# Where the loads of a scan's first constants stand: one recurrence's start-up, re-queued

## The reference, cut to what matters

```python
xr, gate = jnp.split(x @ W_in.T, 2, axis=-1)
xc = silu(causal_conv(xr + t_emb[:, None, :]) + b_conv)
xn = layernorm(xc) * ln_g + ln_b
Bm, Cm, dt = jnp.split(xn @ W_xproj.T, 3, axis=-1)
dt = jnp.tanh(dt @ W_dt.T + b_dt) * 0.01
Ad = 1.0 + dt * -jnp.tanh(A_log)
Bd = Bm * jnp.minimum(jnp.linalg.norm(xn, axis=-1, keepdims=True), 1.0)
def step(h, inputs):                       # 1024 steps, h is 16 x 1024 per batch
    ad, bd, xt, ct = inputs
    h = jnp.clip(h * ad[:, :, None] + bd[:, :, None] * xt[:, None, :], -10.0, 10.0)
    return h, jnp.einsum('bd,bdh->bh', ct, h)
_, ys = jax.lax.scan(step, h0, ...)
x = x + (ys + D * xn) * silu(gate) @ W_out.T
x = x + attention_layer(x, cond_2048)
```

## Time and profile before

| what | us |
| --- | --- |
| median of 3 runs | 3259.34 |
| the profiled execution | 3254.8 |
| its span on the core | 3252.3 |
| VectorE busy in the span | 2189.3 |
| TensorE busy in the span | 2970.4 |
| pre-phase's last instruction on VectorE ends | about 576 |
| first step of the scan on VectorE | 651.24 |
| last step of the scan on VectorE ends | about 1730 |

### The profile page before, as it was taken

How to read it: one execution, slowest core, us unless ns; L and a number is a source line. 1 busy time by engine, 2 the same in 40 slices (tenths; PEclk the granted TensorE clock), 3 DMA queues, 4 the chain that set the end, 5 groups by cost and what they waited for, 6 DMA issues and landing times. The chain is left out here.

```text
span 3252.3 us, 55510 instructions
## 1 busy us (share of the span) xinstructions
PE 2970.4 (91%) x20298; PEld 1402.0 (43%) x20298; DVE 2189.3 (67%) x3124; ACT 1125.2 (35%) x1944; POOL 1135.5 (35%) x464
## 2 busy tenths in 40 slices
PE   6788887099999999999997899996999999999999
PEld 3455556033444444444443576664333333333334
DVE  3767675288889898988987244335777777777714
ACT  3555455011111111111111222121666666666630
POOL 0111112012333343333332111100666777777740
PEclk9888786588999999999998999997999999999999
DMA  2223425534556555555554344336424353535255
GB/s 68 110 101 129 150 104 185 129 77 108 146 144 155 143 148 149 146 150 152 147 145 162 112 150 152 124 128 180 104 75 105 97 128 89 130 92 131 85 184 173
DMA packets 249290, 421.87 MB, mean 130 GB/s; under 512 B 51832, under 2 KB 118008, under 8 KB 242760
## 3 DMA queue, kind: packets, MB, share of 16 engines
q1 hardware_dynamic: 167832, 326.81, 32.9%
q10 hardware_dynamic: 81328, 93.42, 12.4%
HBM read 258.87 MB, written 160.98 MB: 129 GB/s over the span
## 5 line engine op out<-in xcount | busy, mean ns | idle before, releaser
L734 DVE CUSTOM_DVE_ANT_0 b_h<-b_h,b_bx,b_bounds_all 128x256 f32<-128x256 f32 x2048 | 966.3, 540 | 118.0 <-PE b_bx L838 117.5
L1358 DVE TENSOR_REDUCE e_half_max<-ef_banks 128x4 f32<-128x2048 f32 x256 | 586.1, 2293 | 232.7 <-PE ef_banks L1311 232.6
L1501 POOL TENSOR_TENSOR e_pair_sum<-e_probs 128x2048 f32<-128x2048 f32 x128 | 586.8, 4584 | 263.3 <-PE ef_banks L1350 213.9
L1470 ACT ACTIVATE e_probs<-ef_banks 128x512 f32<-128x512 f32 x1024 | 556.1, 595 | 308.9 <-PE ef_banks L1325 308.7
L1325 PE MATMUL ef_banks<-e_qs,e_ks 97*128 97x512 f32 x1024 | 381.7, 452 | 4.0 <-DVE e_half_max L1358 3.6
L848 PE MATMUL b_y_psum<-b_h,b_c_weights 128*32 128x128 f32 x8224 | 339.7, 284 | 4.0 <-ACT b_y_stage L888 4.0
L838 PE MATMUL b_bx<-b_x_moving,b_b_weights 24*128 24x512 f32 x1024 | 262.4, 508 | 69.5 <-POOL b_c_weights L824 58.7
L888 ACT COPY b_y_stage<-b_y_psum 128x128 f32<-128x128 f32 x256 | 68.1, 266 | 721.7 <-PE b_y_psum L848 718.6
L768 PE MATMUL b_gate<-b_w_gate,b_x_tile 128*128 128x512 f32 x512 | 298.6, 666 | 0.0
L1325 PEld LDWEIGHTS ef_banks<-e_qs,e_ks 97*128 97x128 f32 x1024 | 154.4, 188 | 331.2 <-ACT e_probs L1470 312.7
L838 PEld LDWEIGHTS b_bx<-b_x_moving,b_b_weights 24*128 24x128 f32 x1024 | 96.8, 186 | 449.1 <-DVE b_h L734 389.1
(11 more groups left out here) (176 smaller groups left out, 3248.7 us busy)
## 6 DMA issues: line engine op xcount, KB each, us to landing
b_x_moving<-xn_parts SPq DMA_DIRECT2D x248, 128.0 KB
e_ks<-qk_parts ACTq DMA_DIRECT2D x42, 512.0 KB, 4.8
e_qs<-qk_parts ACTq DMA_DIRECT2D x84, 256.0 KB, 3.5
xn_full<-a_xn SPq DMA_DIRECT2D x32, 512.0 KB, 2.6
xn_parts<-a_hi SPq DMA_DIRECT2D x64, 256.0 KB, 2.4
xn_parts<-a_lo SPq DMA_DIRECT2D x64, 256.0 KB, 2.4
silu_gate<-b_sg ACTq DMA_DIRECT2D x64, 256.0 KB, 3.9
scan_out<-b_y_stage ACTq DMA_DIRECT2D x256, 64.0 KB, 4.3
```

The source lines that it names most:

```text
L734: return nc.vector._custom_dve(bass.dve_ops.TENSOR_ADD_SAT, **operands)
L1358: nc.vector.tensor_reduce(out=half_max[:, u // UNITS % 2, :, r // NH, r % NH], in_=(banks[:, u % 2 * GROUP:(u % 2 + 1) * GROUP] if u < FIR ...
L1470: nc.scalar.activation(probs[:, g % 4, h, :], p_exp[h % 2], ACT.Exp).then_inc(exps, 1)
L1501: nc.gpsimd.tensor_tensor(out=pair_sum[:, t % 2], in0=probs[:, (2 * t) % 4], in1=probs[:, (2 * t + 1) % 4], op=ALU.add).then_inc(paired, 1)
```

## The change

Four edits. In the pre-phase's last call, the 8 stores of B's low part move from SyncE to ScalarE (behind the copy L463). In the scan's first block, ScalarE's queue holds only the first half of `b_x_moving`, the gate's weights, the tile, and the second half of `b_x_moving`, in this order. The rest of B's table is asked for by SyncE as the first thing in the loop's block. The output's weights, `b_ident` and `b_d_row` are asked for by SyncE too, behind iteration 1's loads, for which that iteration is taken out of SyncE's first loop.

```diff
@@ sp_part @@
-                for j, t in enumerate((b_hi, b_lo)):
+                for j, t in enumerate((b_hi, b_lo) if n is not None else (b_hi,)):
                     for q in range(NQ):
                         sp.dma_start(bp[j][q], t[:, q, :].bitcast(f32)).then_inc(states_out, 16)
@@ act_part @@
                 nc.scalar.copy(inverse[:], p_turn[0:STATES, :]).then_inc(inverse_copied, 1)
+                if n is None:
+                    bp = Bp[1, bass.ds(p, 1)].rearrange("o e (q k) d -> q (o k) e d", k=P // PHASES)
+                    act.wait_ge(b_parts_ready, START + p * 2 + 2)
+                    for q in range(NQ):
+                        act.dma_start(bp[q], b_lo[:, q, :].bitcast(f32)).then_inc(states_out, 16)
@@ scan_phase, first block @@
             def _(act):
-                for i in range(2):
-                    load_moving(act, 0, i)
+                load_moving(act, 0, 0)
                 act.dma_start(w_gate[:], ...).then_inc(weights_in, 16)
                 act.dma_start(x_tile[:], I["x_tiles"][0]).then_inc(tile_in, 16)
-                load_bd(act, bd_in, EARLY, SEQ // PHASES * STATES)
-                for dst, src in ((w_out[:], ...), (ident[:], I["ident"]), (d_row[:], ...)):
-                    act.dma_start(dst, src).then_inc(others_in, 16)
+                load_moving(act, 0, 1)
@@ scan_phase, the loop's block @@
             def _(sp):
-                with sp.Fori(1, LAG) as it:
+                load_bd(sp, bd_in, EARLY, SEQ // PHASES * STATES)
+                sp_loop(sp, 1, None)
+                for dst, src in ((w_out[:], ...), (ident[:], I["ident"]), (d_row[:], ...)):
+                    sp.dma_start(dst, src).then_inc(others_in, 16)
+                with sp.Fori(2, LAG) as it:
                     sp_loop(sp, it, None)
```

More of the change, by code:

```diff
@@ L687, in _ @@
             def _(act):
-                for i in range(2):
-                    load_moving(act, 0, i)
+                load_moving(act, 0, 0)
                 act.dma_start(w_gate[:], I["w_in_t"][:, INNER:2 * INNER].rearrange("(k p) n -> p k n", p=P)).then_inc(weights_in, 16)
                 act.dma_start(x_tile[:], I["x_tiles"][0]).then_inc(tile_in, 16)
-                load_bd(act, bd_in, EARLY, SEQ // PHASES * STATES)
-                for dst, src in ((w_out[:], I["w_out_t"].rearrange("(m p) n -> p m n", p=P)), (ident[:], I["ident"]),
-                                 (d_row[:], I["D"].rearrange("(o n) -> o n", o=1).to_broadcast([P, INNER]))):
-                    act.dma_start(dst, src).then_inc(others_in, 16)
+                load_moving(act, 0, 1)
             @block.vector
@@ L904, in _ @@
             def _(sp):
-                with sp.Fori(1, LAG) as it:
+                load_bd(sp, bd_in, EARLY, SEQ // PHASES * STATES)
+                sp_loop(sp, 1, None)
+                for dst, src in ((w_out[:], I["w_out_t"].rearrange("(m p) n -> p m n", p=P)), (ident[:], I["ident"]),
+                                 (d_row[:], I["D"].rearrange("(o n) -> o n", o=1).to_broadcast([P, INNER]))):
+                    sp.dma_start(dst, src).then_inc(others_in, 16)
+                with sp.Fori(2, LAG) as it:
                     sp_loop(sp, it, None)
```

## The result

The changed kernel takes 3237.56 us (median of 5 runs, 3234.65 to 3245.26), the kernel before 3260.74 beside it (5 runs, 3257.66 to 3264.91). The ratio is 0.9934, 95% interval 0.9915 to 0.9952: 21.5 us less, between 16 and 28. The profiled execution is one of 3237.56 us with a span of 3235.1. Against the profiled execution of before it is 17.2 us shorter, and these 17.2 are what the traces can explain: the one of before was 5.9 us under the median of those five runs.

A forecast was written before the change was run, and what follows sets the result against it. Bound: VectorE's 43.8 us wait before the scan, small rows behind large ones on two DMA engines. 4.8 + 19.2 + 0.4 - 0.5 - 1.5 = 22.4 us: profiled 3254.8 to 3232.4, median 3237; range 3228 to 3249.

The forecast's parts named there:

- Two queues store B's parts: Pre-phase's end: SyncE and ScalarE store side by side, gain 4.8 us, bounds 0 to 5.2; rival of shared descriptor generation 0.10.
- The wait in front of the scan: Before the scan: small rows no longer wait behind large ones, gain 19.2 us; rival, start bound by bytes (14.6), chance 0.12.
- the timing up to 621: Scan's first block: loads until 621 kept as before, since the order in ScalarE's queue changes but not its bytes.
- the small rows then run alone in 3 us: From 621, 36 small rows on each of two engines: 3.1 us alone instead of 22.3 us beside large rows.
- ScalarE no longer held at the block's end: End of the scan's first block: ScalarE no longer held issuing `b_ident`, only VectorE counts, gain 0.4 us.
- The late table in front of iteration 1's x: SyncE's queue in the loop: loss 0 to 2 us, taken 0.5; rivals: mild stall 0.07, hard stall 0.03.
- S: Time of the scan's first product, 650.40 in the kernel before; iteration 1's x was needed at S + 33.7.
- The clock: TensorE's granted clock in iterations 1 to 4: loss of 1.8 to 3.4 or gains of 1.8 each; loss of 1.5 taken.

The follow-up runs named there:

- e1: Kernel before with the first edit alone, ScalarE storing B's low part in the pre-phase's last call: 3259.82 us, ratio 1.0000.
- e11: Kernel before with half-size idle TensorE products in iterations 0 to 4 and B's low part stored by ScalarE: 3241.02 us, ratio 0.9943.
- e2: Kernel before with the late part of B's table moved last on ScalarE's queue: 3249.42 us, ratio 0.9960.
- e5: Changed kernel with the second half of iteration 0's x asked for by SyncE, ahead of the late table: 3234.38 us, ratio 0.9914.
- e6: Changed kernel with idle, never-read 128x256 TensorE products in the 8 empty places of iterations 0 to 4: 3222.25 us, ratio 0.9858.
- e12: The kernel of e6 again, timed beside e10 and e11: 3226.42 us, ratio 0.9884.
- e7: The kernel of e6 plus 150 repeats of TensorE's product of zeros in the wait before the scan: 3229.88 us, ratio 0.9888.
- e4: Changed kernel with the late table and the output's weights asked for behind iteration 2's loads: 3263.31 us, ratio 1.0006.
- e3: Changed kernel with full-size idle TensorE products in the 8 empty places of iterations 0 to 4: 3235.39 us, ratio 0.9923.
- e10: Kernel before with half-size idle TensorE products in iterations 0 to 4: 3242.14 us, ratio 0.9938.

## Why the prediction was right

The time was forecast at 3237 and is 3237.56. The total is nearer than its terms deserve.

- **Two queues store B's parts: forecast 4.8 us, measured 4.8** (stage 13.5 to 8.7; 5.1 in e1). This is of the stage. In the total e1 and e11 could not show it.
- **The wait in front of the scan: forecast 19.2, measured 20.0** (56.8 to 36.7). The mechanism, small rows one for one behind large ones on few DMA engines (2.05 at work by the earlier trace rows), holds: in the packets of the kernel before, from 639 to 642, rows of 14336 bytes (0.54 us) and of 2048 (0.08 us) start in turn, and e2 takes 14.9 us off by order alone. Why so few engines are at work there no run shows. The details of what follows were wrong. I let the timing up to 621 stand and the small rows then run alone in 3 us. Instead the first 21 us moved 205 GB/s and not 150 (ScalarE's queue held half the x rows there; that this is the cause was not tried by itself), and then the small rows met x's second half, from 604 to 619 at a DMA share of 0.59. Two errors of some 10 us cancelled; e5 measured the second as 10.
- **ScalarE no longer held at the block's end: forecast 0.4, measured 0.5** (scaling to first product 5.77 and 5.24).
- **The late table in front of iteration 1's x: forecast a stall of 0 to 2, taken 0.5, measured 0.** x was asked for at S + 23.8, had landed at S + 33.6 (worked out: S + 31), and the first product of iteration 1 was at S + 34.9. So 1.3 us of margin were left and not 2.7, behind an iteration 0 of 35.8 us at a clock of 0.74. With idle products of half size iteration 0 was quicker, and TensorE waited: 1.6 us in e6, 2.3 in e12, 3.9 in e7. With x's second half in front of the late table (e5) VectorE stalled for 5.6 us, and in e4 the mechanism cost 25.
- **The clock: forecast a loss of 1.5, measured 11.7.** This is the step that failed. I read iterations 1 to 4 of one execution, saw 32.3 and 34.1, and took these for the two cases there are. The 32.3 is itself misread: its row begins at the iteration's first product and ends at a first step, and from step to step it is 30.6, beside 34.6 for iteration 0 in the same profile. Iterations without an output product go from 30.6 to 42.3 us over these runs, by how many of their gate pieces meet a granted clock of 0.50. That it is the clock, e3 and e6 show: they have the moved loads, and iteration 1 at a clock of 1.00 isn't slow. e4's slow iteration 0 shows that the loads aren't needed for it. The 11.7 is of this pair of executions: by the medians the change gains 21.5 us (16 to 28) where the start gives 25.5, so that about 4 us are lost behind it, with a wide interval, and the forecast had 2.0.
- What made up for it. In profiled executions the forecast was 3254.8 - 22.4 = 3232.4, and 3237.6 was measured: 1.1 us more gained at the start, 9.7 less in the iterations, and 3.4 more in the phases behind the scan, which weren't forecast. I then added 4.5 us, because the profiled execution of before lay that far under its median; the one of after is its median. The hit on the median is this 4.5 against that 5.2, which is luck.

Whether the clock falls more often when the start is earlier, and why it falls where it does, stays open for the kernels without idle products. Iteration 0 or 1 takes about 42 us in the profiles of the changed kernel, e2 and e4, with no wait for x in front of it. It doesn't in those of before and e1, nor, its wait for x taken off, in e5, whose start is the earliest of these. With one profile each, chance isn't excluded. With idle products the low stretch in iteration 1 is seen only behind a wait for x. Between e10 and e12 the start gives 25.8 us; 4.7 are lost in iterations 0 to 5 and 0.6 behind the scan, which makes up, to 0.1 us, the 20.4 by which the profiled executions differ. The medians differ by 15.7, as e10's profiled execution is the slowest of its six runs, 5.2 us over their median, and e12's lies 0.5 over its own.

The best version measured is the changed kernel with half-size idle products: 0.9858 and 0.9884, measured twice, against 0.9934 for the change alone.

## What to carry to other kernels

Look at what lies on the same DMA engines beside a transfer that something waits for, not only at the total share: a few small rows can each pay for a large one of the other queue (0.08 us and 0.54 us here). A load that is moved off the critical start must be placed by its engines and not by its bytes, and not directly in front of a load with a due time; whether there is room for it is asked again whenever the work that hides it gets faster. Where TensorE is half idle, price the granted clock from several executions and take its whole range (30.6 to 42.3 us an iteration here), for it can eat half of a gain that is real (11.7 of 25.5 us in the profiled pair).

## What the runs showed of the hardware

- The issue of the small `b_ident` behind the output's weights was held for 29.22 us before, 22.34 in e2 and 23.39 in e4, where large loads had been asked for on the same queue just ahead of the weights. It took 0.64 in the changed kernel, where 39 us lay between the late table's issue and the weights'.
- Two queues issued eight stores of 64-byte rows each, side by side, in 5.06 to 5.56 us; one queue alone took 5.05 and 5.12 for eight.
- Idle products of 128x256 in half of the pairs were enough for a granted clock of 1.00 through iterations 2 to 4 in all seven runs that had them; full-size ones cost 3.4 us an iteration more.
- Products of zeros from 591.5 to 626.5, at a granted clock of 1.00 from 596.2 on, didn't keep the clock high through the first two iterations (0.93 and 0.83 in e7), with TensorE idle for 3.4 and 3.9 us in front of them.
- The phases behind the scan, with the same instructions in every run, took 1518.2 to 1526.1 us over the fourteen profiles, with TensorE at a granted clock of 0.50 for 79 to 99 us of them.
